# A recurrence, routed experts and three engines: low halves of two experts moved from GpSimd to VectorE, and four pieces of work put in another order

## The reference

```python
xw = einsum('ntd,dh->nth', x, Wx) + b
h[t] = tanh(xw[t] + h[t-1] @ Wh)                    # 32 steps, h[-1] = cond
xn = h * rsqrt(mean(h*h) + 1e-5) * norm_scale       # 1024 tokens x 128
vals, idx = top_k(xn @ wg + bg, 4)                  # 16 experts
gates = softmax(vals), spread to gate_full[token, expert]
a, b = even and odd columns of xn @ w1[e] + b1[e]   # every expert, every token
a, b = min(a, 7), clip(b, -7, 7)
y[e] = (a * sigmoid(1.702 * a) * (b + 1)) @ w2[e] + b2[e]
out = x + h + sum over e of gate_full[:, e] * y[e]
```

## Time and profile before

| | |
|---|---|
| median of 3 runs | 104.98 us (104.61 to 105.01) |
| the profiled execution, its own time | 104.61 us |
| its span (first to last instruction) | 102.5 us |
| instructions | 1858 |
| busy: PE, DVE, ACT, POOL | 94%, 72%, 68%, 73% of the span |
| granted TensorE clock | full in every slice |

### The profile page before, as it was taken

How to read it: one execution, slowest core, us unless ns; L and a number is a source line. 1 busy time by engine, 2 the same in 40 slices (tenths; PEclk the granted TensorE clock), 3 DMA queues, 4 the chain that set the end, 5 groups by cost and what they waited for, 6 DMA issues and landing times.

```text
span 102.5 us, 1858 instructions
## 1 busy us (share of the span) xinstructions
PE 96.4 (94%) x593; PEld 82.1 (80%) x593; DVE 73.4 (72%) x186; ACT 69.8 (68%) x158; POOL 74.5 (73%) x85
## 2 busy tenths in 40 slices
PE   6999959998999999999999899999999999999970
PEld 2657628888999799998999788888878888889750
DVE  0306785979669975898779987858886977969630
ACT  3235977899686884669578767568887988997000
POOL 6000268997296997199575999999999999899400
PEclk9999999999999999999999999999999999999999
DMA  2998950000991006960199201994010000000012
GB/s 66 224 307 294 410 218 0 0 16 29 318 401 74 0 13 181 374 267 0 48 313 381 90 0 45 301 360 171 6 54 0 0 0 0 0 0 6 0 51 51
DMA packets 5001, 12.99 MB, mean 127 GB/s; under 512 B 752, under 2 KB 1792, under 8 KB 4992
## 3 DMA queue, kind: packets, MB, share of 16 engines
q1 hardware_dynamic: 4672, 12.66, 36.1%
q10 hardware_dynamic: 320, 0.21, 0.8%
HBM read 12.28 MB, written 0.59 MB: 126 GB/s over the span
## 4 chain that ended last, share of the span: by engine, by line
PE 41%; POOL 29%; DVE 11%; issue 10%; POOLq 2%; ACT 2%; DVEq 0%
POOL actg L461 14%; POOL act_lo L470 10%; PE psA L913 9%; PE psB L913 7%; PE psY L957 5%; PE psA L890 5%; DVE lin L791 3%; POOL w_lo L477 2%; PE psR L858 2%; DVE act L814 2%; DVE logits L675 2%; PE psY L858 2%; POOLq L86 2%; PE psM L969 2%; PE psY L969 2%
## 5 line engine op out<-in xcount | busy, mean ns | idle before, releaser
L791 DVE TENSOR_SCALAR lin<-psB,one_b1b 128x256 f32<-128x256 f32 (+1 forms) x48 | 25.9, 567 | 10.9 <-PE psB L913 10.9
L588 ACT ACTIVATE psA<-psA,lim_b1a 128x256 f32<-128x256 f32 (+1 forms) x48 | 24.0, 516 | 12.8 <-PE psA L913 12.7
L461 POOL TENSOR_TENSOR actg<-act,gate_cols 128x512 f32<-128x512 f32 x25 | 31.9, 1288 | 0.1
L600 ACT ACTIVATE psA<-psA,limit_col 128x512 f32<-128x512 f32 x32 | 21.1, 659 | 0.8
L913 PE MATMUL psA<-xn_hi,w_hi 128*128 128x256 f32 (+1 forms) x48 | 18.0, 376 | 1.6 <-DVE xn_hi L651 1.0
L814 DVE SCALAR_TENSOR_TENSOR act<-lin,psA 128x512 f32<-128x512 f32 x26 | 17.9, 687 | 1.2 <-DVE lin L791 0.5
L913 PE MATMUL psB<-xn_hi,w_hi 128*128 128x256 f32 (+1 forms) x48 | 15.8, 329 | 0.0
L470 POOL TENSOR_TENSOR act_lo<-actg,act_hi 128x512 fp32r<-128x512 f32 x12 | 15.3, 1295 | 0.4 <-ACT act_hi L552 0.4
L913 PE MATMUL psB<-xn_hi,w_lo 128*128 128x256 f32 (+1 forms) x48 | 15.3, 318 | 0.0
L913 PE MATMUL psB<-xn_lo,w_hi 128*128 128x256 f32 (+1 forms) x48 | 15.3, 318 | 0.0
L913 PE MATMUL psA<-xn_hi,w_lo 128*128 128x256 f32 (+1 forms) x48 | 15.3, 319 | 0.0
(11 more groups left out here) (112 smaller groups left out, 192.2 us busy)
## 6 DMA issues: line engine op xcount, KB each, us to landing
gate_cols<-gate_rows SPq DMA_DIRECT2D x16, 512.0 KB, 5.3
w_sb<-in_w SPq DMA_DIRECT2D x4, 512.0 KB, 7.7
w_sb<-in_w SPq DMA_DIRECT2D x4, 256.0 KB, 8.7
out<-yT SPq DMA_DIRECT2D x3, 128.0 KB, 1.7
wx_x_sb<-in_wx_x SPq DMA_DIRECT2D x1, 320.0 KB, 5.3
wx_x_sb<-in_wx_x SPq DMA_DIRECT2D x2, 128.0 KB, 2.6
small_h<-in_small ACTq DMA_DIRECT2D x1, 105.0 KB, 2.8
gate_rows<-gT SPq DMA_DIRECT2D x4, 16.0 KB, 1.8
```

The source lines that it names most:

```text
L461: nc.gpsimd.tensor_tensor(by_pair(actg[:, u % SUM_DEPTH, w]), by_pair(act[:, u % ACT_DEPTH, w]), gate_block(u, w), ALU.mult).then_inc(actg ...
L588: last = nc.scalar.activation(psA[u % 2][:, o], psA[u % 2][:, o], ACT.Relu, scale=-1.0, bias=lim_b1a[:, e0 + k:e0 + k + 1])
L600: nc.scalar.activation(psA[u % 2][:, 0:w], psA[u % 2][:, 0:w], ACT.Gelu_apprx_sigmoid, scale=-1.0, bias=limit_col[:, :]).then_inc(swish_do ...
L791: last = nc.vector.tensor_scalar(lin[:, v % 2, o], psB[v % 2][:, o], one_b1b[:, e0 + k:e0 + k + 1], LIMIT + 1.0, ALU.add, ALU.min)
```

## The change

Four things. VectorE makes the low half of `p` = 2 (experts 4 and 5) in one instruction, from the high halves that ScalarE still makes; GpSimd keeps `p` = 3 to 7, and has nothing between rstd of tile 1 and the exponentials of pair 0. VectorE's low half stands where `close_gates(0)` stood, and `close_gates(0)` comes in unit 0 between lin and act, as for the other pairs. `gates_halves` stands behind act of its unit, and the statistics of a pair (`stats`), which had stood behind it in units 8 and 12, now follow lin. On TensorE the last of the eight steps is followed by `lay_rstd(0)` and then `x_wx(7)`, where it was `x_wx(7)` and then `lay_rstd(0)`. TensorE's waits for low halves follow the new owner.

```diff
@@ constants
-    W1_DVE = 2
+    W1_DVE, W1_LOW_DVE = 2, 3
@@ def w1_low_count(p, a)
-            return p + 1 if p < W1_DVE else 2 * (p - W1_DVE) + a + 1
+            return p + 1 if p < W1_LOW_DVE else 2 * (p - W1_LOW_DVE) + a + 1
@@ GpSimd
             power_rstd(0)
             power_rstd(1)
-            for a in range(2):
-                w1_low(W1_DVE, a)
             power_expo(0)
             place_expo(0)
-            for p in range(W1_DVE + 1, NP):
+            for p in range(W1_LOW_DVE, NP):
                 for a in range(2):
                     w1_low(p, a)
@@ VectorE
             def w1_halves(p):
-                dve.wait_ge(w1_loaded[2 * p // EG], 16)
                 pe_ = slice(2 * p, 2 * p + 2)
-                mark(nc.vector.tensor_copy(w1_hi[:, pe_, :, :], w1_sb[:, pe_, :, :]))
-                settled()
+                if p < W1_DVE:
+                    dve.wait_ge(w1_loaded[2 * p // EG], 16)
+                    mark(nc.vector.tensor_copy(w1_hi[:, pe_, :, :], w1_sb[:, pe_, :, :]))
+                    settled()
+                else:
+                    dve.wait_ge(w1_hi_ready, 2 * (p - W1_DVE) + 2)
                 nc.vector.tensor_tensor(w1_lo[:, pe_, :, :], w1_sb[:, pe_, :, :], w1_hi[:, pe_, :, :].bitcast(F32),
                                         ALU.subtract).then_inc(w1_ready, 1)
...
             route_hot(0)
-            close_gates(0)
+            w1_halves(W1_DVE)
...
                     last.then_inc(lin_done, 1)
-                for q in at(GATES_T, v - 1):
-                    gates_halves(q)
-                if v == LAST_T + 1:
-                    gates_halves(NQ - 1)
                 for q in at(STATS, v):
                     stats(pair_group(q))
-                if v:
-                    for q in at(GATES, v):
-                        close_gates(q)
+                for q in at(GATES, v):
+                    close_gates(q)
...
+                for q in at(GATES_T, v - 1):
+                    gates_halves(q)
+                if v == LAST_T + 1:
+                    gates_halves(NQ - 1)
                 for q in at(RSTD, v):
                     route_logits(q)
@@ TensorE
                 step(t)
-                if t in XW_GAP:
-                    x_wx(XW_GAP[t], 1, start=False)
                 if t == TL + 1:
                     pe.wait_ge(consts_ready, 1)
                     sums(0).then_inc(m_mm, 1)
                 elif t == HEAD - 1:
                     lay_rstd(0)
+                if t in XW_GAP:
+                    x_wx(XW_GAP[t], 1, start=False)
                 keep_warm(GAP)
...
-                    pe.wait_ge(w1_ready if v < W1_DVE else w1_half_ready, w1_low_count(v, 0))
+                    pe.wait_ge(w1_ready if v < W1_LOW_DVE else w1_half_ready, w1_low_count(v, 0))
...
-                if W1_DVE <= v < UNIT0[1]:
+                if W1_LOW_DVE <= v < UNIT0[1]:
                     pe.wait_ge(w1_half_ready, w1_low_count(v, 1))
```

## The result

The changed kernel takes 103.72 us (median of 5 runs, 103.47 to 104.09) against 104.98 (5 runs, 104.61 to 105.08): a ratio of 0.9884, 95% interval 0.9854 to 0.9914, so 1.2% faster. The forecast was 104.2, range 103.5 to 104.7. The profiled execution took 103.47 with a span of 101.4, 1.1 shorter than before; 2.1 lie around the span, as before.

What follows compares the result with a forecast made beforehand. Bound: a head to 14.89 us, a stretch passed among TensorE, ScalarE and VectorE, then a GpSimd tail from 55.00. 1.00 + 0.13 - 0.38 = 0.75 to 0.80 us saved, from the median 104.2; range 103.5 to 104.7.

Steps and rivals of the forecast that it cites:

- part 5: Pair 1's logits on VectorE newly meet GpSimd's second gate product and are kept out: cost 0.38 us, bounds 0 and 0.6.
- (a): Rival: no new meeting of pair 1's logits with GpSimd's product, gain 1.00 + 0.13, time 103.85; chance 0.27.
- (b): Rival: the moves of VectorE's gate work are worth 0.3 to 0.5 us more, time 103.4; chance 0.08.
- Part 1: Head: tile 0's transpose goes ahead of the last x product on TensorE; gain 0.15 us, bounds 0 and 0.30.
- Part 2: Head: without GpSimd's low halves of unit 2, pair 0's logits take 0.39 not 1.27; 1.0 us earlier, 0.15 from Part 1.
- Part 3: Unit 0: VectorE's low half and new order delay pair 0's inverse and ScalarE's scaling; cost 0.20 us, bounds 0.1 and 0.35.
- (c): Rival: GpSimd's exponential keeps out VectorE's low half, some 0.9 of the 1.0 us is lost, 104.9; chance 0.08.
- (d): Rival: VectorE's low half loses every turn to GpSimd's exponential, product and first half of unit 3; 0.7 slower, 105.7; chance 0.04.
- (e): Rival: GpSimd does not cause pair 0's stretched logits; only 0.15 us is won and given back, 104.9; chance 0.07.
- Part 4: Unit 2: gate halves behind act spare TensorE's wait before unit 4; some 0.13 us kept, bounds 0 and 0.3; other pairs nothing.

Runs made afterwards that it cites:

- x_first: The changed kernel with the last x product back ahead of tile 0's transpose on TensorE; 103.78 us.
- low_later: The kernel before with only GpSimd's two low halves of unit 2 moved behind its gate product of pair 0, none on VectorE; 103.76 us.
- order_only: The changed kernel with unit 2's low halves back on GpSimd at their old place, none on VectorE, all changes of order kept; 104.31 us.
- halves_first: The changed kernel with the halves of the transposed gates back ahead of statistics and act in units 2, 8, 12 and 17; 103.79 us.
- cols_late: The changed kernel with pair 0's gate columns requested only when step 15 of the recurrence is done; 104.34 us.
- Low_later_order: The changed kernel with unit 2's low halves made by GpSimd behind its gate product of pair 0, none on VectorE; 102.99 us, 103.43 when run again.
- transpose_later: Low_later_order with ScalarE scaling pair 0's gates behind unit 1's Relus and TensorE transposing them behind unit 1's second step; 103.29 us.

## Why the prediction was right, and where it was not

The time fell within the range, and the order of the hand-overs was right: a saving in the head passes to the end undiminished. The single number, 104.2, was 0.5 too high, most of it by the 0.38 charged in part 5; it is the range, wide enough to take in rivals (a) and (b), that held. By its own steps:

**Part 1**, 0.15: measured 0.15 (x_first).

**Part 2**, 0.85 on top of it, the logits held by GpSimd's low halves: measured 0.90 (low_later), 3.87 to 2.82 with part 1 together, 1.05 against the 1.00 of the sum. The mechanism is shown twice, by moving the halves away and by taking one SBUF input from the logits while the halves stayed.

**Part 3**, a cost of 0.20 through ScalarE's chain: 0.16 between order_only and the changed kernel. That the low half lies safely beside GpSimd's exponential was right: it took 0.68 there. The cited section, read plainly, would have had it wait; the row of the changed kernel disagrees, as the one-hot row did. Rivals (c) and (d) fall with that row, and (e) with both logits experiments. The chain by which the 0.16 is lost is seen in the traces: ScalarE idles 0.54 for the inverse where it idles 0.36 in order_only, and TensorE's next step comes 4.67 behind unit 0 instead of 4.49.

**Part 4** kept 0.13 behind part 3's loss of 0.20, so it took the move by itself for 0.33: it measured 0.35 (halves_first), and 20.05 to 19.89, 0.16, remain of parts 3 and 4. Rival (b), 0.3 to 0.5 more from the moves, falls with that. The moved pairs of units 8, 12 and 17 changed nothing: the two later distances of the table are the same.

**Part 5** is the step that failed. It charged 0.38 for a meeting of the logits of pair 1 with GpSimd's second product. The rule holds, as cols_late shows; the input did not. It put the first product at the landing of the gate columns and took that landing from the one profile, behind a write of 3.5 us. It left out GpSimd's own work ahead of the product, rstd of pair 1. This is its row in the first profile of the kernel before:

```profile
27.40 0.71 POOL L414 TENSOR_TENSOR rstd<-meansq,neg_half 128x2 f32<-128x2 f32 x1 [2.33 <-DVE raw L643]
```

It ends at 28.11, so even there the landing (28.07, product at 28.23) held the product by only 0.12 to 0.15. In the changed kernel the write took 2.0, the columns landed 4.3 behind their request, at 26.4 and ahead of rstd's end at 27.01, and the product followed rstd. In 12 of the 14 profiles it does, in the second one of the kernel before too; the other two are the first profile and cols_late. Without the charge the sum is 1.13, which is rival (a), 103.85; measured were 1.21 in the traces and 1.26 between the medians. The chance split, 0.42 for the meeting and 0.27 against, leaned on a single transfer's latency that I had myself seen to spread: the four writes of that line in the first profile landed after 1.4 to 3.5, with a median of 1.8, and pair 0's was the slowest.

**A version that beats both** came from the question who has to make the low half at all: nobody has to make it in the head. Low_later_order keeps the changed order and leaves the halves to GpSimd, later: 87.36 in the sum of distances, against 87.53 and 88.74; transpose_later, 87.29, is not to be told from it. Against the changed kernel this rests on the distances in the traces, since the runs do not separate the two.

## What to carry to other kernels

When an operation with small work takes far longer than its siblings, look at what the other engines do in just that time: VectorE with two SBUF inputs waited nearly to the end of GpSimd's low halves and products (though not of its exponentials), here 0.9 us in the head, and the cheapest cure was to start GpSimd's work later, not to give it to another engine. Before you charge for two pieces of work that will meet, ask which row sets each one's start; where it is the landing of a single small transfer, take the spread of its landings and not the one value, and look for work of the same engine that ends at about the same time. And compare distances between marks in the traces, since these showed 0.15 us cleanly where the runs of one kernel spread by a whole microsecond.

## What the runs showed of the hardware that I had not expected

In the second profile of the kernel before, TensorE's granted clock fell right behind the start of unit 0. The windows of that execution; the number behind the five busy times is the granted clock.

```profile
12.00:14.00 2.00, 1.43 (x8) 0.43 (x7) 1.42 (x5) 2.00 (x7) 1.80 (x3) 1.00 0.87 332
...
14.00:16.00 2.00, 1.42 (x8) 1.45 (x8) 1.86 (x13) 0.40 (x2) 0.68 (x2) 0.68 0.09 32
...
16.00:18.00 2.00, 2.00 (x12) 2.00 (x11) 0.87 (x5) 1.65 (x4) 1.92 (x4) 0.50 0.00 0
...
18.00:20.00 2.00, 2.00 (x19) 2.00 (x18) 1.48 (x4) 1.73 (x6) 2.00 (x4) 0.97 0.04 8
```

It was at its full level (2.4 GHz) to 14 us, at half (1.2 GHz) from 16 to 18, and back by about 18. Ahead of the fall TensorE had stood idle 1.0 us for xn_hi of tile 1, up to 14.58. The stretch from unit 0 to pair 1's transposes was 20.66 there against 20.05 in the first profile, whose clock never fell though it had the same idle microsecond. The changed kernel, without that idle time, kept the clock in both of its profiles. The mean clocks of the runs say more. Of the 60 runs of the kernel before in the three later sessions 11 had 0.983 or 0.984, as this execution had; their median is 105.14 against 104.78 of the other 49. None of the 97 runs of all the other kernels was below 0.994. But order_only has the idle microsecond too and kept its clock in 12 runs, so the idle time seems to be needed (not shown) and does not suffice; what decides it is open, and no run here was made for it. The time of that execution, 104.92, does not stand out, since its head began 0.3 earlier.
